# The end of a fused attention and mixture-of-experts kernel gets an instruction order of its own on every engine

## The reference

```python
h = _layernorm(x) * (1 + ca) + sa
x = x + ga * attention(h)              # 16 heads of width 8, vals @ Wo.T + bo
h = _layernorm(x) * (1 + cb) + sb      # the second half starts here
...
logits = h @ router_w.T                # 8 experts
probs = softmax(logits)
topk_vals, topk_idx = top_k(probs, 2)
topk_w = topk_vals / (topk_vals.sum(-1, keepdims=True) + 1e-06)
expert_out = einsum('nh,eho->eno', h, expert_weights)
out = ((expert_out[top] + topk_vals) * topk_w).sum(over the two)
x = x + gb * out
```

## Time and profile before

| what | value |
|---|---|
| median of 3 runs | 565.9 us (565.25 to 566.61) |
| the profiled execution, its own time | 566.31 us |
| its span, first to last instruction | 564.5 us |
| mean granted TensorE clock | 0.981 |
| busy in the span: PE, ACT, DVE, POOL | 92%, 86%, 64%, 40% |

### The profile page before, as it was taken

How to read it: one execution, slowest core, us unless ns; L and a number is a source line. 1 busy time by engine, 2 the same in 40 slices (tenths; PEclk the granted TensorE clock), 3 DMA queues, 4 the chain that set the end, 5 groups by cost and what they waited for, 6 DMA issues and landing times.

```text
span 564.5 us, 14303 instructions
## 1 busy us (share of the span) xinstructions
PE 521.4 (92%) x4046; PEld 215.1 (38%) x4046; DVE 363.8 (64%) x1276; ACT 487.7 (86%) x546; POOL 223.2 (40%) x436
## 2 busy tenths in 40 slices
PE   7489899999999999999999999999999999998753
PEld 6233333343443434333343433434343343333232
DVE  4435367666777676666677767666776776664464
ACT  1389999999999999999999999999999999999600
POOL 1222333444444433343444443334444444323337
PEclk9999999999999999999999999999999999999966
DMA  4473333333333333333233333333333333330100
GB/s 100 125 203 91 97 78 88 93 100 80 74 92 89 90 87 94 97 91 83 72 87 91 89 87 89 98 97 86 81 75 88 91 89 91 94 95 24 26 15 14
DMA packets 85496, 48.43 MB, mean 86 GB/s; under 512 B 61508, under 2 KB 76240, under 8 KB 85456
## 3 DMA queue, kind: packets, MB, share of 16 engines
q1 hardware_dynamic: 70468, 43.18, 30.1%
q10 hardware_dynamic: 14988, 4.72, 3.7%
HBM read 32.91 MB, written 14.94 MB: 85 GB/s over the span
## 4 chain that ended last, share of the span: by engine, by line
PE 82%; ACT 9%; DVE 3%; POOL 2%; issue 2%; DMA 1%; SPq 0%; ACTq 0%; POOLq 0%; DVEq 0%
PE ps_attn L677 42%; PE ps_scores L659 21%; ACT probs L523 9%; PE ps_side L707 8%; PE ps_side L597 4%; PE ps_side L604 2%; PE ps_side L613 1%; PE ps_side L690 1%; PE ps_side L591 1%; PE ps_side L694 1%; PE ps_side L584 1%; PE ps_scores L707 1%; DMA wqkv_in<-in_L_attn_Wqkv_dram 0%; POOL mix L459 0%; DVE weighted L1073 0%
## 5 line engine op out<-in xcount | busy, mean ns | idle before, releaser
L523 ACT ACTIVATE probs<-ps_scores 128x1024 f32<-128x1024 f32 x512 | 485.7, 1028 | 41.9 <-DMA q_scr<-qk_parts 19.7
L677 PE MATMUL ps_attn<-probs,values 128*32 128x512 f32 x2048 | 248.4, 599 | 0.2 <-issue 0.2
L659 PE MATMUL ps_scores<-query_stack,key_stack 32*128 32x512 f32 x1024 | 130.8, 500 | 16.5 <-ACT probs L523 10.9
L659 PEld LDWEIGHTS ps_scores<-query_stack,key_stack 32*128 32x128 f32 x1024 | 49.4, 183 | 166.9 <-ACT probs L523 162.2
L412 POOL TENSOR_SCALAR var_eps<-moments 128x1 f32<-128x1 f32 x64 | 12.2, 191 | 231.1 <-DVE moments L1004 158.9
L677 PEld LDWEIGHTS ps_attn<-probs,values 128*32 128x32 f32 x2048 | 54.1, 109 | 110.6 <-issue 110.6
L707 PE MATMUL ps_side<-experts_gated,h2T 128*128 (+1 forms) x228 | 74.7, 409 | 0.0
L993 DVE RECIPROCAL sums_inv<-sums 128x128 f32<-128x128 f32 x32 | 30.4, 951 | 33.6 <-DMA attnT<-a_scr 33.6
L1073 DVE TENSOR_TENSOR weighted<-ps_side,coef 128x256 f32<-128x256 f32 x114 | 46.5, 408 | 2.4 <-PE ps_side L707 2.4
L1000 DVE TENSOR_TENSOR x<-ps_side,x_gated 128x128 f32<-128x128 f32 x30 | 8.7, 292 | 59.8 <-PE ps_side L707 56.0
L459 POOL TENSOR_TENSOR mix<-weighted 128x512 f32<-128x512 f32 x32 | 40.9, 1278 | 0.0
(11 more groups left out here) (119 smaller groups left out, 507.3 us busy)
## 6 DMA issues: line engine op xcount, KB each, us to landing
key_stack<-k_scr SPq DMA_DIRECT2D x128, 128.0 KB, 2.7
query_stack<-q_scr SPq DMA_DIRECT2D x121, 64.0 KB, 2.3
q_scr<-qk_parts SPq DMA_DIRECT2D x188, 32.0 KB, 2.0
k_scr<-qk_parts SPq DMA_DIRECT2D x64, 64.0 KB, 1.7
a_scr<-attn ACTq DMA_DIRECT2D x124, 18.0 KB
sums<-a_scr SPq DMA_DIRECT2D x32, 64.0 KB, 2.2
attnT<-a_scr SPq DMA_DIRECT2D x32, 64.0 KB, 2.3
out_dram<-out_all ACTq DMA_DIRECT2D x28, 64.0 KB, 1.9
```

The lines of the kernel that those rows point to most:

```text
L523: nc.scalar.activation(probs[:, k % RING, g, :], ps_scores[:, slot(k, g), :], ACT.Exp, scale=SCALE)\
L659: mm = nc.tensor.matmul(out_, key_stack[p0:p0 + 32, parity, 2 * k:2 * k + 2, :].rearrange("p j r -> p (j r)"), query_stack[p0:p0 + 32, par ...
L677: mm = nc.tensor.matmul(ps_attn[q:q + 32, :], values[:, parity, g, k, :], probs[:, k % RING, g, h * HALF:(h + 1) * HALF], start=(k == 0), ...
```

## The change

The loop body stays as it is, but for its last pass: ACT takes the router exponential of tile 29 between the last two exponentials of `probs`, and VectorE does the router of tile 29 (top two, weights, `base`) at the end of that pass. `router_tail` and `c_router_weights` are each cut in two functions, which the loop calls one after the other.

Behind the loop each engine has a list of its own instead of the four passes:

- ACT copies the attention of tile 31 out of `ps_attn` and issues two of its four writes (SP the other two). It weighs ten pieces (tile 28's last two, all of tiles 29 and 30), and two of the four of tile 31. A piece is two instructions of 128x128 with a column of `coef` as scale. It stores the last tile.
- VectorE weighs the other two pieces of tile 31 and, for that tile, computes `coef` and adds up the eight experts itself, in `mix_last`. It does the router of tile 30 before it takes the reciprocal for tile 31.
- POOL keeps the other adds. PE uses `ps_side` and `ps_attn` for the side products, and six banks for the experts, numbered in `TAIL_BANKS`. It runs nine products without use (`keep_warm`) around the projection of tile 31.

```diff
-            write_attn(sp, T, range(4))
+            write_attn(sp, T, (2, 3))
...
-            for past in range(4):
-                tile(T + past, past % 2, 4, -1, past)
+            router_tail(T - 2)
+            rstd(T - 1, moments2, var_eps2, rstd2, "moments2_done", "var2_done", "rstd2_done")
+            router_coef(T - 2)
+            gated_x(T - 1, T)
+            mix_eight(T - 3, 0)
+            mix_two(T - 4, T - 3, 0)
+            router_tail(T - 1)
+            router_coef(T - 1)
+            rstd(T, moments2, var_eps2, rstd2, "moments2_done", "var2_done", "rstd2_done")
+            mix_eight(T - 2, 1)
+            mix_two(T - 3, T - 2, 1)
+            mix_eight(T - 1, 0)
+            mix_two(T - 2, T - 1, 0)
...
+                        if after == 0 and k == KT - 1 and g == 0:
+                            router(t - 1)
...
+            def weigh(y, piece):
+                y1, ring, ps, (e0, e1) = y + 1, y % 2, tail_bank(TAIL_BANKS[y, piece]), PIECES[piece]
+                reached(act, experts_done[piece], y1)
+                reached(act, ev["coef_done"], y1)
+                reached(act, ev["mix4_done"], y1 - 2)
+                for e in range(e0, e1):
+                    ins = nc.scalar.activation(weighted[:, ring, e, :], ps[:, 4 * P - (e1 - e) * D:4 * P - (e1 - e - 1) * D], ACT.Copy,
+                                               scale=coef[:, e:e + 1])
+                ins.then_inc(weighted_done[piece], 1)
...
+            save()
+            write_attn(act, T, (0, 1))
+            weigh(T - 4, 2)
+            weigh(T - 4, 3)
+            weigh(T - 3, 0)
+            weigh(T - 3, 1)
+            weigh(T - 3, 2)
+            router(T - 1)
+            weigh(T - 3, 3)
+            for piece in range(4):
+                weigh(T - 2, piece)
+            router(T)
+            weigh(T - 1, 2)
+            weigh(T - 1, 3)
+            store_last()
...
+                reached(pe, weighted_done[1], T - 3)
+                c_project(ps_side, T - 1, (T - 2) // TB)
+                experts(T - 4, 2)
+                experts(T - 4, 3)
+                experts(T - 3, 0)
+                experts(T - 3, 1)
+                c_transpose(ps_side[:, P:2 * P], T - 1)
+                experts(T - 3, 2)
+                experts(T - 3, 3)
+                c_logits(ps_side[:, P:3 * P], T - 1, 0)
...
+                keep_warm(4, tail_bank(5)[:, 0:P])
+                reached(pe, ev["attn_saved"], T)
+                c_project(ps_attn, T, (T - 1) // TB)
+                keep_warm(5, tail_bank(5)[:, 0:P])
+                c_transpose(ps_attn[:, P:2 * P], T)
+                c_logits(ps_attn[:, P:3 * P], T, 1)
...
             def last():
-                for past in range(4):
-                    tile([tail_bank(past, n) for n in range(4)], T + past, past % 2, 4, -1, past)
+                c_x1(ps_side, T - 1, 0)
+                c_x1hat(T - 1, 0)
+                c_h2T(ps_side[:, P:2 * P], T - 2, T - 1, 0)
+                c_logits(ps_side[:, P:3 * P], T - 1)
+                c_router_top(T - 1)
+                c_vals(T)
+                c_router_weights(T - 1)
+                c_x1(ps_attn, T, 1)
+                c_router_base(T - 2, T - 1, 0)
+                c_x1hat(T, 1)
+                c_h2T(ps_attn[:, P:2 * P], T - 1, T, 1)
+                c_logits(ps_attn[:, P:3 * P], T)
+                c_router_top(T)
+                c_router_weights(T)
+                c_coef(T)
+                for piece in range(2):
+                    c_weigh(tail_bank(TAIL_BANKS[T - 1, piece]), T, 1, piece)
+                c_router_base(T - 1, T, 1)
+                mix_last()
```

More of the change, by code:

```diff
@@ L387, in _ @@
             tiles(sp, tile)
-            write_attn(sp, T, range(4))
+            write_attn(sp, T, (2, 3))
             read_attn(T)
-            for y in range(T - 4, T):
+            for y in range(T - 4, T - 1):
                 store(sp, y + 1, y)
@@ L481, in tile @@
                 if past < 3 <= before:
-                    router_tail(plus(pool, t, -2), 1 - parity)
+                    router_tail(plus(pool, t, -2))
+                    router_coef(plus(pool, t, -2))
                 if past < 4 <= before:
@@ L535, in _, with save, store_last, keep_warm @@
             read_q(act, 1, 0, (0, 1, 2))
-            tiles(act, tile)
-            for y1 in range(T - 2, T + 1):
-                router(y1)
+            def weigh(y, piece):
[7 more added lines that the diff above has]
+                ins.then_inc(weighted_done[piece], 1)
+            def save():
+                reached(act, pv_done[KT - 1], T)
+                reached(act, a_written, 64 * (T - 1))
+                nc.scalar.activation(attn[:].rearrange("p j r -> p (j r)"), ps_attn[:], ACT.Copy).then_inc(ev["attn_saved"], 1)
+            def store_last():
+                reached(act, out_last, 1)
+                act.dma_start(out_tiles[T - 1], out_all[:, T - 1, :]).then_inc(out_stored, 16)
+            tiles(act, tile)
+            save()
[13 more added lines that the diff above has]
+            store_last()
         @block.tensor
         def _(pe):
-            def keep_warm(n):
+            def keep_warm(n, dst=ps_scores[:, 0, 0:P]):
                 for _ in range(n):
-                    nc.tensor.matmul(ps_scores[:, 0, 0:P], ident[:], ident[:], start=True, stop=True)
+                    nc.tensor.matmul(dst, ident[:], ident[:], start=True, stop=True)
             def modulation(chunk):
@@ L1125, in tile @@
                     exact_maxima(t, at[1], parity)
-                if after < 0 and past < 1:
-                    c_save(t)
                 written0(at, before, after, past)
@@ L1181, in tile @@
                     c_weigh(banks[3], at[-2], 1 - parity, 1)
-                if after < 0 and past < 1:
-                    c_vals(t)
-            def tail_bank(past, n):
-                bank = (4 * past + n) % (2 * SLOTS)
-                return ps_scores[:, bank // 2, (bank % 2) * HALF:(bank % 2 + 1) * HALF]
-            def last():
-                for past in range(4):
-                    tile([tail_bank(past, n) for n in range(4)], T + past, past % 2, 4, -1, past)
+                if after == 0:
+                    c_router_top(t - 1)
+                    c_router_weights(t - 1)
+                    c_router_base(t - 2, t - 1, parity)
@@ new lines, in c_coef @@
+            def c_coef(y1):
+                reached(dve, weighted_done[3], y1 - 1)
+                reached(dve, ev["pair_w_done"], y1)
+                v.tensor_scalar(coef0[:], expert_ids[:], top_idf[:, 0:1], pair_w[:, 0:1], ALU.is_equal, ALU.mult)\
+                    .then_inc(ev["coef0_done"], 1)
+                v.tensor_scalar(coef1[:], expert_ids[:], top_idf[:, 1:2], pair_w[:, 1:2], ALU.is_equal, ALU.mult)\
+                    .then_inc(ev["coef1_done"], 1)
+                reached(dve, ev["coef0_done"], y1)
+                reached(dve, ev["coef1_done"], y1)
+                v.tensor_tensor(coef[:], coef0[:], coef1[:], ALU.add).then_inc(ev["coef_done"], 1)
@@ new lines, in mix_last @@
+            def mix_last():
+                reached(dve, weighted_done[0], T)
+                reached(dve, weighted_done[1], T)
+                v.tensor_tensor(tail_pairs[:, 0], weighted[:, 1, 0:2, :], weighted[:, 1, 2:4, :], ALU.add)\
+                    .then_inc(ev["tail_mix_done"], 1)
+                reached(dve, weighted_done[2], T)
+                reached(dve, weighted_done[3], T)
+                v.tensor_tensor(tail_pairs[:, 1], weighted[:, 1, 4:6, :], weighted[:, 1, 6:8, :], ALU.add)\
+                    .then_inc(ev["tail_mix_done"], 1)
+                reached(dve, ev["tail_mix_done"], 2)
+                v.tensor_tensor(tail_four[:], tail_pairs[:, 0], tail_pairs[:, 1], ALU.add).then_inc(ev["tail_mix_done"], 1)
+                reached(dve, ev["tail_mix_done"], 3)
+                v.tensor_tensor(tail_sum[:], tail_four[:, 0, :], tail_four[:, 1, :], ALU.add).then_inc(ev["tail_mix_done"], 1)
+                reached(dve, ev["tail_mix_done"], 4)
+                reached(dve, ev["base_done"], T)
+                v.tensor_tensor(out_all[:, T - 1, :], base[:, 1, :], tail_sum[:], ALU.add).then_inc(out_last, 1)
```

61 lines of the change are left out of this document (37 added, 24 removed).

## The result

The changed kernel takes 557.68 us (median of 5 runs, 556.68 to 558.22) against 566.08 us of the kernel before (5 runs, 565.25 to 566.84) in the same comparison: ratio 0.9856, 95% interval 0.9844 to 0.9869. Forecast were 556.9 us and a range of 555.0 to 560.2. The profiled execution took 557.98 us, with a span of 556.1 us, where 564.5 stood.

What follows compares the result with a forecast made beforehand. Behind the loop nothing is full: the end is a chain of waits. Span 564.5 to 555.5, 9.0 us less (2.2 from earlier `valsT`, the rest behind it); 557.3 for the profiled execution, median 0.4 lower: 556.9 us, range 555.0 to 560.2.

Steps and rivals of the forecast that it cites:

- its own list of signs: Things to see in the trace; wrong if ScalarE's instruction exceeds 0.5, the clock falls or the loop ends after 533.3.
- The loop: Last pass: moved exponential costs nothing (0.21 us uncovered); VectorE's router of tile 29 runs from about 531.2 to 533.7.
- Tile 30: Behind the loop: `x1` at 533.79, transposition 0.45, logits 0.40, exponential done at 538.46, router at 539.8.
- ScalarE's weighing: Pieces weighed at the end: 0.31 us per 128x128 instruction; with 0.6 the sum moves by 3.4 us.
- rivals 4 and 5: ScalarE's weighing instruction costs about 0.6 us (time 560.3, chance 0.12) or 1.03 us (time 569.7, chance 0.02).
- The transfers: Tile 31's attention: `attnT` lands about 538.9, VectorE gets to it at 539.7; landing 0.8 us later still covered.
- Rival 6: The end is not shortened, as transfers rather than VectorE's order bind `valsT` of tile 31: time 565 to 566, chance 0.03.
- The new wait at `x1hat`: Tile 31: POOL's 1.26 us add holds `x1hat`, which ends 0.08 after it, at 544.74 and not 543.81.
- rival 2: Fewer collisions as VectorE slips ahead of POOL at `x1hat` and in the router; all gone: time 555.3, chance 0.12.
- Collisions in the router: Tile 31's router: `router_p`, `pair_sum` and the like caught by POOL's adds, 0.45 us.
- rival 3: TensorE falls to 1.2 GHz in the end, from tile 30's transposition on: time 560.4, chance 0.13.
- VectorE's adds: Tile 31's last adds: 0.41 us for 256 columns, 0.29 for 128, the last ending at 553.46.

Runs made afterwards that it cites:

- the second variant: Changed kernel with POOL waiting for `x1hat` of tile 31 before tile 29's adds and for `coef` of tile 31 before tile 30's: 556.75 us, ratio 0.9838.
- the first variant of POOL's waits: Changed kernel with POOL waiting for `x1hat` of tile 31 before tile 29's adds: 557.46 us, ratio 0.9837.
- third variant of POOL's waits: As the second variant, with `coef` of tile 30 also put behind `rstd` of tile 31 on POOL: 556.53 us, ratio 0.983.

## Why the prediction was right, step by step

The mechanism and nearly all sizes held. The end was forecast at 22.2 and took 21.96. In the profiled execution the time was 0.7 us above the 557.3 forecast for it: the loop ended 0.9 later than the 533.3 that had been taken for it, less the 0.24 of the end. That the medians (556.9 and 557.68) differ by 0.8 for the same reason is likely and not shown, as only one execution has a trace. By its own list of signs two things spoke against the prediction: the loop ended later than 533.3, and the clock fell before 547. Neither touched the mechanism of the end.

The end also came out closer than its terms. Up to `router_exp` of tile 31 the kernel was 0.32 ahead of the forecast, the router and `coef` took 0.27 more than forecast, and from there to the last add it was 0.19 less: together the 0.24. That the first two nearly cancel is luck.

- **The loop.** The moved exponential costs nothing that can be seen: TensorE is busy for 3.30 of 3.30 us with it, and the changed kernel and the eleven variants that keep it ended the loop between 531.8 and 534.5, on both sides of the 533.3 before. On VectorE the router of tile 29 let `x1` of tile 30 start 0.46 behind the product (forecast 0.49). Without the move it is 1.2 us more.
- **Tile 30** was 0.3 us faster up to `router_exp` (4.84, forecast 5.16). The transposition took 0.33 and not 0.45, the logits 0.28 and not 0.40.
- **ScalarE's weighing** was sized well: eight in 2.18 and four in 1.14 us, so (2.18 - 1.14)/4 = 0.26 for each that follows; a single one takes 0.36 to 0.41 by itself. The estimate was 0.31 for each. That leaves rivals 4 and 5 (0.6 and 1.03) no room. The sensitivity held as well: issued twice, which is about 0.5 for each, the weighing cost 3.62 us, where the sum had 3.4 for 0.6. The Trainium skill (ScalarE: Activation LUTs, What ACT_TABLE_LOAD costs) gives 186 ns and 0.833 ns for a column, 93 more for a pointer operand and 93 of overlap between neighbours: an estimate by it is 0.39 us alone and 0.29 in a row. The runs agree for one alone and show slightly less in a row.
- **The transfers** were covered as forecast: the reciprocal starts without idle time behind `pair_eps`, and the run with all writes on SyncE, once its collision is removed, ends within 0.07 us of the changed kernel. The forecast had them landing 5.6 behind the product with 0.8 us to spare; they landed at 5.7 with 0.5 to spare, since VectorE came sooner. Rival 6 falls with it.
- **The new wait at `x1hat`** came as worked out: 1.28 us long, ending 0.08 behind POOL's add, `x1hat` at 11.27 (11.4). POOL was ahead by 0.06 us, so rival 2 did not happen. What the step did not say is that the 0.93 us cannot be had by letting POOL wait: the next of POOL's adds then holds a CAST for just as long.
- **Collisions in the router** were priced at 0.45 and measured 0.33 (`router_p`) and 0.26 (`pair_sum`), 0.59 together; up to the end of `coef` 0.1 more was lost than forecast. All collisions of tile 31 together cost 1.6 us, the number given for the case without blocking.
- **The clock.** It stayed at 1.00 until 546.55, where 536 to 547 had been asked. From there on nearly all products of tile 31's experts ran at 0.50, off the chain, as the last of them ended at 550.25 and `coef` at 550.84. So the clock did fall, but not where rival 3 had it. Without the extra products it fell 4 us earlier, and the end was the same, since POOL's add hides 0.27 us of delay; the nine products, to which the prediction gave a part in holding the clock, were worth nothing in time. What rival 3 priced, a fall from tile 30's transposition on, no run shows: in all kernels with the new order the clock was still at 1.00 there.
- **VectorE's adds** took 0.42 a pair, 0.43, 0.29 and 0.29: from the end of `coef` to the last add 3.27 us, forecast 3.46.

## What to carry to other kernels

When a pipelined loop drains, its order is made for work that no longer comes: find for each late tile what its instruction stands behind on its own engine, and write the end in the order of the last tile's chain. Before buying a wait that avoids a collision, look for the next instruction that will be in the same place, because two lists that shift together collide again. A delay that ends inside a wait costs nothing, so measure a fix by the end of the chain and not by the step that it shortens.

## What the runs showed of the hardware

**Which instructions POOL holds.** Beside POOL's adds (TENSOR_TENSOR with both operands in SBUF), VectorE's TENSOR_SCALAR, CAST and TENSOR_TENSOR of two SBUF operands were held to the end of the add, small ones as long as large ones: a TENSOR_SCALAR of 128x128 took 1.28 instead of 0.35, a CAST of 128x8 1.24 instead of 0.16, a TENSOR_TENSOR of 128x1 0.40 instead of 0.14. There are exceptions. `pair_eps`, a TENSOR_SCALAR of 128x1, started at 540.28, 0.03 behind an add, and took its 0.15; and a TENSOR_TENSOR of 128x1 at 534.08, beside POOL's TENSOR_SCALAR for `coef`, took its 0.16. Not held either were the RECIPROCAL at 540.34 (0.94 us beside an add from 540.25 to 540.71; 0.95 in the earlier trace rows) and the weighing at 551.38 in the kernel before, which reads PSUM, 0.42. It works the other way too: POOL's add at 551.06 in the second variant took 0.72 instead of 0.46 beside VectorE's adds. The Trainium skill (SBUF — State Buffer, Who interferes with whom) says that the shared pair of ports goes to whoever issues first, for the whole instruction. The traces agree that one of the two waits for the other's end, and that 0.05 us at the start can decide 1.1 us. The starts in the rows don't always tell which: with all writes on SyncE `router_p` started at 538.53, 0.05 ahead of POOL's add, and was held all the same (0.53), while in the second variant of POOL's waits an add of VectorE at 551.05, 0.01 ahead of POOL's, took its 0.41 and POOL's was held.

**Runs differ in the first tile.** The end behind the product repeats well: `x1` of tile 30 starts at 0.46 in the changed kernel and in both runs with SyncE's writes, and `coef` of tile 31 ends at 16.65 and 16.67 in the changed kernel and the first variant of POOL's waits. What moves between runs lies ahead. ScalarE issues reads of `query_stack` between two of the first exponentials. The timeline of ScalarE before:

```profile
31.79 1.63 ACTq L294 DMA_DIRECT2D query_stack<-q_scr  x2
33.53 2.86 ACT L523 ACTIVATE probs<-ps_scores 128x1024 f32<-128x1024 f32 x3 [1.07 <-PE ps_scores L659]
```

and in the changed kernel:

```profile
32.41 2.29 ACTq L304 DMA_DIRECT2D query_stack<-q_scr  x2
34.81 1.94 ACT L547 ACTIVATE probs<-ps_scores 128x1024 f32<-128x1024 f32 x2 [2.48 <-issue]
```

Two issues of the same transfers take 1.63 us in one execution and 2.29 in the other (1.26 to 2.31 over all profiled kernels), the two before them 1.19 and 1.95, and the exponential behind them starts 1.3 us later, in code that the change doesn't touch. The 0.9 us by which the loop ended later in the profiled execution has about this size. That it is the whole of it was not shown: over the profiled kernels the end of the loop follows these times only loosely. The 0.9 is larger than every difference between the variants with an end of 21.6 to 22.4 us, so their medians (556.0 to 557.7) don't rank them, and neither the second nor the third variant of POOL's waits is shown to beat the changed kernel.
